# Layer statistics from one interleaved pass, and the first residual made by VectorE straight from PSUM

## The chip, the cores and the metric

The kernel runs on one core of a Trainium2 chip. The metric is the device time of one execution in microseconds (us). In the texts and profile rows PE is TensorE's matrix multiply and PEld its weight load, DVE is VectorE, ACT is ScalarE, POOL is GpSimd, SP is SyncE.

## What is computed

A batch of 32 graphs, each with 256 nodes of 256 features, goes through four graph layers. Each layer has a residual and a layer norm over the 256 features of a node:

```
x = _layernorm(x + _L0_gnn_ref(x, adj, W, b))            # adj @ (x W + b), divided by the row sums of adj
x = _layernorm(x + _L1_gnn_ref(x, adj, kernel))          # relu((adj @ x) kernel) * mask
x = _layernorm(x + _L2_gnn_ref(x, adj, kernel, bias))    # relu(normalized (adj + I) @ x kernel + bias)
x = _layernorm(x + _L3_gnn_ref(x, adj, Wv, bv, aw, ab, Wk, bk))   # attention weights, two hops, relu

def _layernorm(x, axis=-1, eps=1e-05):
    m = jnp.mean(x, axis=axis, keepdims=True)
    v = jnp.var(x, axis=axis, keepdims=True)
    return (x - m) / jnp.sqrt(v + eps)
```

So each graph needs a mean and a variance per node four times, once per layer.

## The kernel before

A graph lies in SBUF as a tile of 128 partitions by C = 512 columns: each partition holds two nodes, node t = 0 in columns 0 to 255 and node t = 1 in columns 256 to 511. `nodes(tile)` is that tile seen as (partition, t, feature). Four graphs, the slots g = 0 to 3, are in flight together, and eight groups of four follow each other. Products are made to nearly full precision from a high and a low half of every operand (`_hi`, `_lo`), three matmuls for each pair: ACT copies the high half out, and DVE or POOL subtracts it to get the low half.

The order of the work is written out by hand, separately for each engine: `first_iteration()`, then a loop over `iteration(k)`, which does layers 2 and 3 of group k interleaved with layers 0 and 1 of group k + 1 (and the first product of group k + 2), and then `last_iteration(k)`. Every engine runs its list strictly in order, and semaphores join the engines. An engine also waits on a semaphore of its own where an operation reads what one shortly before has written (`st_ready`, `mv_ready`, `rinv0_ready`, `z2_ready`).

PSUM holds four `ring` tiles, one per slot, and two `pair` tiles of two banks each. PE writes layer 0's second product (`s2`) of slot g into `pair[g % 2]`, with column F holding the row sums of adj. `s2` of slots 2 and 3, `s8a` and `s8b` of slot 0 (layer 3) and the first `s1` products write the same banks again, and so must wait until layer 0's result has been taken out of them. Before the change ACT's `z0` takes it out.

The steps around the change, per slot:

- **Layer 0's residual.** DVE `sums0` (L993, L994) takes the row sums and their reciprocal `rinv`. ACT `z0` (L495) reads the product from `pair`, scales it by `rinv` and writes X1, two operations of 256 columns. POOL `y0` (L759) adds X1 to X0, one operation of 512 columns.
- **Statistics, for each of the four layers.** DVE `statistics` (L975): two `bn_stats` of 256 columns, one per node, 6 words each. DVE `moments` (L982): two `bn_aggr`, which join those words to mean and variance. DVE `variance_eps` (L987, L988): adds eps and negates the mean. Then POOL `power` (L766) raises to -0.5, and POOL or ACT normalizes.
- Other names in the rows: `from_ring` (L966), `h_lo_part` (L970), `xd_lo` (L1020), `x1_lo` (L1015), `alpha_lo_part` (L998) and `p2_lo` (L1002) make low halves; `leaky` is L1041, `mask_of_x1` L1006, `y1`, `y2b` and `y3` (L1011, L1033, L1067) are the other residuals; `q` (L1054), `y2` (L1028) and `z3` (L1062) are products taken from PSUM with a per-node scale, two operations of 256 columns.

## Time and profile before

| | us |
|---|---|
| median of 3 runs (609.42 to 612.31) | 609.57 |
| the profiled execution's own time | 607.73 |
| its span, first to last instruction | 605.7 |

| engine | busy us | share of the span | instructions |
|---|---|---|---|
| PE | 544.7 | 90% | 4044 |
| PEld | 512.8 | 85% | 4044 |
| DVE | 557.7 | 92% | 1597 |
| ACT | 425.2 | 70% | 937 |
| POOL | 466.8 | 77% | 575 |

Busy time is the time in which an engine has an instruction open. DVE and PE instructions overlap their neighbours' ends, so what an instruction takes out of its engine's time is the distance from its start to the next one's start, which the view in order of time shows. A stretch of the loop repeats every 70.5 us; the rows below use seven such stretches.

### The profile page before, as it was taken

Reading aid. Unit: us, or ns where it says so; the run is one execution under the profiler, and the core shown is the slowest. Engines: PE = TensorE matmul, PEld = TensorE weight load, DVE = VectorE, ACT = ScalarE, POOL = GpSimd, SP = SyncE. Lnnn points to the kernel's source line nnn. Section 1 sums busy time; section 2 is a strip of 40 time slices with the busy share of each in tenths; the row PEclk is TensorE's granted clock in tenths of the full one; section 3 lists DMA queues with packets and bytes.
Section 4 is the critical chain, followed back from the end, with each engine's and each line's share of the span. In section 5 each row is a group of like instructions: output and inputs, shape, how many; then the busy total and the mean of one; then the engine's idle time right before and its main releaser. Section 6 shows DMA issues by size and latency. Waiting matters only on the chain.

```text
span 605.7 us, 12633 instructions
## 1 busy us (share of the span) xinstructions
PE 544.7 (90%) x4044; PEld 512.8 (85%) x4044; DVE 557.7 (92%) x1597; ACT 425.2 (70%) x937; POOL 466.8 (77%) x575
## 2 busy tenths in 40 slices
PE   5688999999989999999998999899999999987983
PEld 5577988999889988999888999899889998886873
DVE  3789999999999999999999999999999999999766
ACT  5467887488856878578873878658785778756653
POOL 3798789788987789878897788977898787873243
PEclk9979999999999999999999999999999999999998
DMA  8623101430132300323014211313003200101001
GB/s 291 221 59 112 41 18 46 142 120 25 35 104 69 139 17 17 113 95 104 17 49 125 104 52 35 104 69 139 17 17 106 102 36 2 54 18 70 1 1 69
DMA packets 25223, 44.73 MB, mean 74 GB/s; under 512 B 3184, under 2 KB 3824, under 8 KB 25200
## 3 DMA queue, kind: packets, MB, share of 16 engines
q1 hardware_dynamic: 24336, 43.79, 22.0%
q10 hardware_dynamic: 864, 0.66, 0.3%
q8 instruction: 12, 0.20, 0.1%
q14 instruction: 11, 0.09, 0.1%
HBM read 36.05 MB, written 8.39 MB: 73 GB/s over the span
## 4 chain that ended last, share of the span: by engine, by line
DVE 56%; PE 28%; issue 7%; POOL 4%; DMA 2%; ACT 2%; DVEq 0%; ACTq 0%; POOLq 0%
DVE stats L975 10%; PE pair L259 6%; DVE nod_lo L1020 5%; PE pair L261 5%; PE pair L260 5%; PE ring L259 4%; DVE ring L1062 4%; DVE fea_lo L966 4%; PE ring L261 4%; PE ring L260 4%; DVE P L1054 4%; DVE powin L987 3%; DVE tmp L1041 3%; DVE X L1067 3%; DVE nod_lo L1015 3%
## 5 line engine op out<-in xcount | busy, mean ns | idle before, releaser
L766 POOL TENSOR_TENSOR rstd<-powin,minus_half 128x2 f32<-128x2 f32 (+1 forms) x128 | 105.0, 821 | 71.1 <-DVE nmean L988 71.1
L565 ACT ACTIVATE X<-X,nmr,rstd 128x256 f32<-128x256 f32 x192 | 103.7, 593 | 33.8 <-POOL nmr L775 33.7
L975 DVE BATCH_NORM_STATS2 stats<-X 128x6 f32<-128x256 f32 x256 | 94.3, 411 | 1.6 <-POOL X L759 1.2
L259 PE MATMUL ring<-adj_hi,nod_lo 128*128 128x256 f32 x256 | 74.8, 292 | 12.8 <-DVE X L1067 8.2
L259 PE MATMUL ring<-W_hi,fea_lo 128*128 128x256 f32 x256 | 72.4, 283 | 1.5 <-DVE fea_lo L966 1.4
L260 PE MATMUL ring<-adj_lo,nod_hi 128*128 128x256 f32 x256 | 72.8, 285 | 0.0
L261 PE MATMUL ring<-adj_hi,nod_hi 128*128 128x256 f32 x256 | 72.8, 284 | 0.0
L261 PE MATMUL ring<-W_hi,fea_hi 128*128 128x256 f32 x256 | 71.7, 280 | 0.0
L260 PE MATMUL ring<-W_lo,fea_hi 128*128 128x256 f32 x256 | 71.4, 279 | 0.0
L486 ACT ACTIVATE fea_hi<-ring 128x512 fp32r<-128x512 f32 x96 | 54.9, 588 | 16.5 <-PE ring L321 11.3
L486 ACT ACTIVATE h_hi<-P 128x512 fp32r<-128x512 f32 x32 | 20.3, 633 | 65.7 <-DVE P L1054 65.7
L966 DVE TENSOR_TENSOR fea_lo<-ring,fea_hi 128x512 fp32r<-128x512 f32 x96 | 63.3, 679 | 1.8 <-ACT fea_hi L486 1.8
L259 PEld LDWEIGHTS ring<-adj_hi,nod_lo 128*128 128x128 f32 x256 | 49.2, 192 | 16.2 <-DVE nod_lo L1020 11.9
L259 PE MATMUL pair<-WB_hi,fea_lo 128*128 128x512 f32 x128 | 53.6, 419 | 9.5 <-DVE h_lo L1002 9.5
L788 POOL TENSOR_TENSOR tmp<-tmp,adj_in 128x512 f32<-128x512 f32 x32 | 44.0, 1385 | 14.2 <-ACT tmp L550 14.2
L796 POOL TENSOR_TENSOR h_lo<-P,h_hi 128x512 fp32r<-128x512 f32 x32 | 39.3, 1229 | 17.5 <-ACT h_hi L486 16.7
L261 PE MATMUL pair<-WB_hi,fea_hi 128*128 128x512 f32 x128 | 50.7, 396 | 0.0
L260 PE MATMUL pair<-WB_lo,fea_hi 128*128 128x512 f32 x128 | 50.7, 396 | 0.0
L781 POOL TENSOR_SCALAR X<-X,nmean,rstd 128x256 f32<-128x256 f32 x64 | 45.8, 725 | 5.7 <-POOL rstd L766 5.7
L259 PEld LDWEIGHTS ring<-W_hi,fea_lo 128*128 128x128 f32 x256 | 48.2, 188 | 2.4 <-issue 1.3
L754 POOL TENSOR_TENSOR adj_lo<-adj_in,adj_hi 128x512 fp32r<-128x512 f32 x32 | 40.8, 1293 | 11.7 <-ACT adj_hi L486 11.7
L261 PEld LDWEIGHTS ring<-adj_hi,nod_hi 128*128 128x128 f32 x256 | 49.5, 193 | 0.0
(110 smaller groups left out, 2166.2 us busy)
## 6 DMA issues: line engine op xcount, KB each, us to landing
adj_in<-adjT_dram SPq DMA_DIRECT2D x64, 256.0 KB, 3.2
xT_in<-xT_dram SPq DMA_DIRECT2D x32, 256.0 KB, 3.5
X<-x_dram SPq DMA_DIRECT2D x32, 256.0 KB, 2.6
out_dram<-X SPq DMA_DIRECT2D x32, 256.0 KB, 2.0
P<-wk_dram SPq DMA_DIRECT2D x3, 256.0 KB, 8.1
P<-w_dram SPq DMA_DIRECT2D x2, 256.0 KB, 7.8
X<-bk_dram SPq DMA_DIRECT2D x3, 128.0 KB, 7.8
P<-w_dram ACTq DMA_DIRECT2D x1, 256.0 KB, 3.8
```

The source lines that it names most:

```text
L259: mm(o, lhs(1, t, i), rhs(0, t), start=t == 0, stop=False)
L260: mm(o, lhs(0, t, i), rhs(1, t), start=False, stop=False)
L261: last = mm(o, lhs(0, t, i), rhs(0, t), start=False, stop=t == 1)
L486: return nc.scalar.activation(dst, src, ACT.Copy)
L565: last = nc.scalar.activation(nodes(X[min(l + 1, 3)][g])[:, t, :], nodes(X[l][g])[:, t, :], ACT.Identity, scale=rstd[l][g][:, t:t + 1], bi ...
L754: tt(adj_lo[g][:, :], adj_in[g][:, :], adj_hi[g][:, :], ALU.subtract).then_inc(adj_ready, 1)
L766: tt(rstd[l][g][:, 0:n], powin[l][g][:, 0:n], minus_half[:, 0:n], ALU.pow).then_inc(rstd_ready[l], 1)
L781: last = ts(nodes(X1[g])[:, t, :], nodes(X0[g])[:, t, :], nmean[0][g][:, t:t + 1], rstd[0][g][:, t:t + 1], ALU.add, ALU.mult)
L788: tt(tmp[g][:, :], tmp[g][:, :], adj3_in[g][:, :], ALU.mult).then_inc(al_ready, 1)
L796: tt(mixed(h_lo[g])[:, :, 0:F], nodes(P1[g]), mixed(h_hi[g])[:, :, 0:F], ALU.subtract).then_inc(Q_lo_ready, 1)
L966: tt(fea_lo[g][:, :], ring[g][:, :], fea_hi[g][:, :], ALU.subtract).then_inc(ready, 1)
L975: last = nc.vector.bn_stats(stats[l][g][:, 6 * t:6 * t + 6], nodes(X[l][g])[:, t, :])
```

## The change

`by_turns(tile)` shows the two nodes of a tile interleaved: feature 0 of node 0, feature 0 of node 1, feature 1 of node 0, and so on. One `bn_stats` over those 512 columns writes six words: count, mean and sum of squared deviations of its elements with even numbers, and the same three of those with odd numbers. With this view the even ones are node 0 and the odd ones node 1, so nothing has to be joined: `moments` is gone, and `variance_eps` reads the words directly, with the division by F in the operation that adds eps. Layer 0's residual becomes `y0` on DVE, two operations per slot that multiply the PSUM product by `rinv` and add X0 in place; ACT's `z0` and POOL's `y0` are gone, and PE waits for `y0_done` where it waited for `z0_ready`.

```diff
+        def by_turns(tile):
+            return tile[:, 0:C].rearrange("p (t f) -> p f t", t=2)
...
             def s2(g, kn):
...
                 if g >= 2:
-                    pe.wait_ge(z0_ready, count(g - 2, kn))
+                    pe.wait_ge(y0_done, count(g - 2, kn))
...
-            def z0(g, kn):
-                act.wait_ge(rinv0_ready, count(g, kn))
-                for t in range(2):
-                    last = nc.scalar.activation(nodes(X1[g])[:, t, :], pair[g % 2][:, t, 0:F], ACT.Identity,
-                                                scale=rinv[g][:, t:t + 1])
-                last.then_inc(z0_ready, 1)
...
-            def y0(g, kn):
-                pool.wait_ge(xb_ready, count(g, kn))
-                pool.wait_ge(z0_ready, count(g, kn))
-                tt(X0[g][:, :], X0[g][:, :], X1[g][:, :], ALU.add).then_inc(y_ready[0][g], 1)
...
             def statistics(l, g, k):
-                dve.wait_ge(y_ready[l][g], k + 1)
-                for t in range(2):
-                    last = nc.vector.bn_stats(stats[l][g][:, 6 * t:6 * t + 6], nodes(X[l][g])[:, t, :])
-                last.then_inc(st_ready[l], 1)
-
-            def moments(l, g, k):
+                if l == 0:
+                    dve.wait_ge(y0_done, count(g, k))
+                else:
+                    dve.wait_ge(y_ready[l][g], k + 1)
+                nc.vector.bn_stats(stats[l][g][:, :], by_turns(X[l][g])).then_inc(st_ready[l], 1)
+
+            def variance_eps(l, g, k):
                 dve.wait_ge(w0_ready, 1)
                 dve.wait_ge(st_ready[l], count(g, k))
-                for t in range(2):
-                    last = nc.vector.bn_aggr(mv[l][g][:, 2 * t:2 * t + 2], stats[l][g][:, 6 * t:6 * t + 6])
-                last.then_inc(mv_ready[l], 1)
-
-            def variance_eps(l, g, k):
-                dve.wait_ge(mv_ready[l], count(g, k))
-                ts(powin[l][g][:, 0:2], mv[l][g][:, 1:4:2], EPS, None, ALU.add)
-                ts(nmean[l][g][:, :], mv[l][g][:, 0:4:2], -1.0, None, ALU.mult).then_inc(nm_ready[l], 1)
+                ts(powin[l][g][:, 0:2], stats[l][g][:, 2:6:3], 1.0 / F, EPS, ALU.mult, ALU.add)
+                ts(nmean[l][g][:, :], stats[l][g][:, 1:6:3], -1.0, None, ALU.mult).then_inc(nm_ready[l], 1)
...
+            def y0(g, kn):
+                dve.wait_ge(rinv0_ready, count(g, kn))
+                dve.wait_ge(xb_ready, count(g, kn))
+                for t in range(2):
+                    half = nodes(X0[g])[:, t, :]
+                    last = stt(half, pair[g % 2][:, t, 0:F], rinv[g][:, t:t + 1], half, ALU.mult, ALU.add)
+                last.then_inc(y0_done, 1)
```

In the lists of work all 128 calls of `moments` go (32 graphs, four layers), and the calls of `z0` and of POOL's `y0` go. DVE's `y0(g, k + 1)` stands a few places behind `sums0(g, k + 1)`. The rest of every list keeps its order.

The part of DVE's loop in which layer 2 of group k and layer 0 of group k + 1 begin, before (`powin<-pair` and `rinv<-pair` are `sums0`, `ring<-ring,rstd` is `y2`, `X<-ring,X` is `y2b`, the number behind a name is the slot):

```order
L982 BN_AGGR mv_0<-stats_0 128x2 x2
L993 TENSOR_SCALAR powin_0<-pair 128x2
L994 RECIPROCAL rinv<-pair 128x2
L987 TENSOR_SCALAR powin_0<-mv_0 128x2
L988 TENSOR_SCALAR nmean_0<-mv_0 128x2
L1028 SCALAR_TENSOR_TENSOR ring<-ring,rstd_1,b_bc 128x256 x2
L1028 SCALAR_TENSOR_TENSOR ring<-ring,rstd_2,b_bc 128x256 x2
L1033 SCALAR_TENSOR_TENSOR X_1<-ring,X_1 128x512
L993 TENSOR_SCALAR powin_1<-pair 128x2
L994 RECIPROCAL rinv<-pair 128x2
L975 BN_STATS stats_1<-X_1 128x6 x2
```

The same part with the change:

```order
L961 TENSOR_SCALAR powin_0<-pair 128x2
L962 RECIPROCAL rinv<-pair 128x2
L955 TENSOR_SCALAR powin_0<-stats_0 128x2
L956 TENSOR_SCALAR nmean_0<-stats_0 128x2
L969 SCALAR_TENSOR_TENSOR X_0<-pair,rinv,X_0 128x256 x2
L1004 SCALAR_TENSOR_TENSOR ring<-ring,rstd_1,b_bc 128x256 x2
L1004 SCALAR_TENSOR_TENSOR ring<-ring,rstd_2,b_bc 128x256 x2
L1009 SCALAR_TENSOR_TENSOR X_1<-ring,X_1 128x512
L961 TENSOR_SCALAR powin_1<-pair 128x2
L962 RECIPROCAL rinv<-pair 128x2
L950 BN_STATS stats_1<-X_1 128x6
L969 SCALAR_TENSOR_TENSOR X_1<-pair,rinv,X_1 128x256 x2
```

The joins `BN_AGGR` are gone, a `BN_STATS` stands once where it stood twice, and `X<-pair,rinv,X` (the new `y0`) stands ahead of the next slots' `y2` (slot 0) and behind the statistics that follow `sums0` (slot 1).

The part of DVE's loop in which layers 2 and 0 of the later slots meet, before (`P<-pair,bk_bc` is layer 3's `p0`, `nod_lo` is `x1_lo`):

```order
L975 BN_STATS stats_1<-X_1 128x6 x2
L1033 SCALAR_TENSOR_TENSOR X_3<-ring,X_3 128x512
L1015 TENSOR_TENSOR nod_lo<-X_0,nod_hi 128x512
L975 BN_STATS stats_3<-X_3 128x6 x2
L1037 TENSOR_TENSOR P_1<-pair,bk_bc 128x516
L1002 TENSOR_TENSOR h_lo<-pair,h_hi 128x2x256
L982 BN_AGGR mv_3<-stats_3 128x2 x2
L982 BN_AGGR mv_1<-stats_1 128x2 x2
L987 TENSOR_SCALAR powin_3<-mv_3 128x2
L988 TENSOR_SCALAR nmean_3<-mv_3 128x2
```

With the change:

```order
L950 BN_STATS stats_1<-X_1 128x6
L1009 SCALAR_TENSOR_TENSOR X_3<-ring,X_3 128x512
L991 TENSOR_TENSOR nod_lo<-X_0,nod_hi 128x512
L950 BN_STATS stats_3<-X_3 128x6
L1013 TENSOR_TENSOR P_1<-pair,bk_bc 128x516
L978 TENSOR_TENSOR h_lo<-pair,h_hi 128x2x256
L955 TENSOR_SCALAR powin_3<-stats_3 128x2
L956 TENSOR_SCALAR nmean_3<-stats_3 128x2
```

Two `BN_AGGR` rows of two operations each are gone between the low half `h_lo` and the eps operation; no operation has come in here.

POOL's list at the start of the loop, before (`rstd` is `power`, `nmr` is `mean_scale`, `X<-X,nmean,rstd` is `norm0`):

```order
L775 TENSOR_TENSOR nmr_0<-nmean_0,rstd_0 128x2
L759 TENSOR_TENSOR X_0<-X_0 128x512
L754 TENSOR_TENSOR adj_lo<-adj_in,adj_hi 128x512
L766 TENSOR_TENSOR rstd_1<-powin_1,minus_half 128x2
L775 TENSOR_TENSOR nmr_1<-nmean_1,rstd_1 128x2
L759 TENSOR_TENSOR X_1<-X_1 128x512
L766 TENSOR_TENSOR rstd_0<-powin_0,minus_half 128x4
L781 TENSOR_SCALAR X_0<-X_0,nmean_0,rstd_0 128x256 x2
```

With the change:

```order
L756 TENSOR_TENSOR nmr_0<-nmean_0,rstd_0 128x2
L740 TENSOR_TENSOR adj_lo<-adj_in,adj_hi 128x512
L747 TENSOR_TENSOR rstd_1<-powin_1,minus_half 128x2
L756 TENSOR_TENSOR nmr_1<-nmean_1,rstd_1 128x2
L747 TENSOR_TENSOR rstd_0<-powin_0,minus_half 128x4
L762 TENSOR_SCALAR X_0<-X_0,nmean_0,rstd_0 128x256 x2
```

The two `X<-X` additions (`y0` of slots 0 and 1) are gone, so that `power` of layer 0 follows at once on `mean_scale` of layer 2's slot 1.

## Rows read from the trace of the kernel before

**Rows 1.** The page: span, busy time of each engine, chain by engine.

```profile
span 605.7 us, 12633 instructions
...
PE 544.7 (90%) x4044; PEld 512.8 (85%) x4044; DVE 557.7 (92%) x1597; ACT 425.2 (70%) x937; POOL 466.8 (77%) x575
...
DVE 56%; PE 28%; issue 7%; POOL 4%; DMA 2%; ACT 2%; DVEq 0%; ACTq 0%; POOLq 0%
```

**Rows 2.** Windows, one a loop turn: busy us (count) of each engine.

```profile
core 0: us, PE busy (x) PEld busy (x) DVE busy (x) ACT busy (x) POOL busy (x), PEclk, DMA share, GB/s
...
247.20:317.70 70.50, 66.69 (x506) 63.26 (x505) 68.11 (x197) 52.30 (x116) 59.50 (x73) 1.00 0.23 74
...
sum 493.30, PE 465.37 PEld 439.50 DVE 474.43 ACT 366.29 POOL 412.76; mean PE 66.48 PEld 62.79 DVE 67.78 ACT 52.33 POOL 58.97
```

**Rows 3.** Lines of DVE by form: count | busy us, mean ns | idle before.

```profile
L975 DVE BATCH_NORM_STATS2 stats<-X 128x6 f32<-128x256 f32 x256 | 94.3, 411 | 1.6 <-POOL X L759 1.2
L966 DVE TENSOR_TENSOR fea_lo<-ring,fea_hi 128x512 fp32r<-128x512 f32 x96 | 63.3, 679 | 1.8 <-ACT fea_hi L486 1.8
...
L987 DVE TENSOR_SCALAR powin<-mv 128x2 f32<-128x2 f32 x128 | 35.0, 273 | 1.1
...
L982 DVE BATCH_NORM_AGGREGATE mv<-stats 128x2 f32<-128x6 f32 x256 | 29.7, 158 | 3.2 <-issue 0.2
...
L1054 DVE SCALAR_TENSOR_TENSOR P<-pair,rinv,P 128x256 f32<-128x256 f32 x64 | 27.6, 471 | 0.4
```

**Rows 4.** The same view, more operations with every operand in SBUF.

```profile
L1020 DVE SCALAR_TENSOR_TENSOR nod_lo<-X,rstd,nod_hi 128x256 fp32r<-128x256 f32 x64 | 46.2, 763 | 0.5 <-ACT nod_hi L527 0.4
...
L1041 DVE SCALAR_TENSOR_TENSOR tmp<-tmp 128x512 f32<-128x512 f32 x32 | 31.1, 972 | 1.5 <-ACT tmp L544 0.6
...
L998 DVE TENSOR_TENSOR alpha_lo<-tmp,alpha_hi 128x512 fp32r<-128x512 f32 x32 | 29.2, 928 | 0.0
L1015 DVE TENSOR_TENSOR nod_lo<-X,nod_hi 128x512 fp32r<-128x512 f32 x32 | 28.4, 889 | 2.1 <-ACT nod_hi L486 2.1
...
L1006 DVE TENSOR_SCALAR mask<-absum 128x2 f32<-128x2 f32 x32 | 13.1, 410 | 0.0
```

**Rows 5.** DVE in order of time, 285 to 296 us: start us, us, operation.

```profile
285.57 0.23 DVE L982 BATCH_NORM_AGGREGATE mv<-stats 128x2 f32<-128x6 f32 x2
285.72 0.12 DVE L993 TENSOR_SCALAR powin<-pair 128x2 f32<-128x2 f32 x1
...
286.12 0.74 DVE L975 BATCH_NORM_STATS2 stats<-X 128x6 f32<-128x256 f32 x2
286.78 0.86 DVE L1028 SCALAR_TENSOR_TENSOR ring<-ring,rstd,b_bc 128x256 f32<-128x256 f32 x2
287.55 0.23 DVE L982 BATCH_NORM_AGGREGATE mv<-stats 128x2 f32<-128x6 f32 x2
287.82 0.23 DVE L987 TENSOR_SCALAR powin<-mv 128x2 f32<-128x2 f32 x1
...
289.89 0.67 DVE L1033 SCALAR_TENSOR_TENSOR X<-ring,X 128x512 f32<-128x512 f32 x1
290.48 1.50 DVE L1015 TENSOR_TENSOR nod_lo<-X,nod_hi 128x512 fp32r<-128x512 f32 x1
...
294.78 0.74 DVE L975 BATCH_NORM_STATS2 stats<-X 128x6 f32<-128x256 f32 x2
295.62 0.25 DVE L982 BATCH_NORM_AGGREGATE mv<-stats 128x2 f32<-128x6 f32 x2
295.79 0.81 DVE L987 TENSOR_SCALAR powin<-mv 128x2 f32<-128x2 f32 x1
```

**Rows 6.** POOL in order of time, 290 to 296 us.

```profile
290.15 1.29 POOL L759 TENSOR_TENSOR X<-X 128x512 f32<-128x512 f32 x1
...
295.28 1.29 POOL L759 TENSOR_TENSOR X<-X 128x512 f32<-128x512 f32 x1
```

**Rows 7.** Waits over the whole span: total us, times, longest.

```profile
PE pair L259 <- ACT X L495: 4.6, 2, 2.3
```

More of the change, by code:

```diff
@@ L87, in build @@
         alpha_hi, alpha_lo = slots("alpha_hi", C, FR), slots("alpha_lo", C, FR)
-        stats = [slots(f"stats{l}_", 12) for l in range(4)]
-        mv = [slots(f"mv{l}_", 4) for l in range(4)]
+        stats = [slots(f"stats{l}_", 6) for l in range(4)]
         nmean = [slots(f"nmean{l}_", 2) for l in range(4)]
@@ L114, in build @@
         h_hi_ready, h_ready = sem("h_hi_ready"), sem("h_ready")
-        deg_ready, z0_ready = sem("deg_ready"), sem("z0_ready")
-        y_ready = [sem4(f"y{l}_ready") for l in range(4)]
+        deg_ready, y0_done = sem("deg_ready"), sem("y0_done")
+        y_ready = {l: sem4(f"y{l}_ready") for l in (1, 2, 3)}
         st_ready = [sem(f"st{l}_ready") for l in range(4)]
-        mv_ready = [sem(f"mv{l}_ready") for l in range(4)]
         nm_ready = [sem(f"nm{l}_ready") for l in range(4)]
@@ L280, in s1 @@
                 elif kn == 1:
-                    pe.wait_ge(z0_ready, count(2 + g // 2, 0))
+                    pe.wait_ge(y0_done, count(2 + g // 2, 0))
                 product([h_bank(g)[:, 0:N], h_bank(g)[:, N:2 * N]], cols((xT_hi, xT_lo), g),
@@ L329, in s8a @@
                 elif not last:
-                    pe.wait_ge(z0_ready, count(2, k + 1))
+                    pe.wait_ge(y0_done, count(2, k + 1))
                 product([pair[0][:, i, 0:FA] for i in range(2)], cols(fea, g),
@@ L337, in s8b @@
                 elif not last:
-                    pe.wait_ge(z0_ready, count(3, k + 1))
+                    pe.wait_ge(y0_done, count(3, k + 1))
                 product([pair[1][:, i, :] for i in range(2)], cols(fea, g),
@@ L814, in first_iteration @@
                     diag_sum(g, 0)
-                y0(0, 0)
                 xT_lo_part(0, 1)
-                for g in (1, 2):
-                    y0(g, 0)
                 xT_lo_part(1, 1)
@@ L824, in first_iteration @@
                 norm0(1, 0)
-                y0(3, 0)
                 power(0, 2, 0)
@@ L857, in iteration @@
                 mean_scale(2, 0, k)
-                y0(0, k + 1)
                 adj_lo_part(3, k + 1)
@@ L861, in iteration @@
                 mean_scale(2, 1, k)
-                y0(1, k + 1)
                 power(0, 0, k + 1)
@@ L867, in iteration @@
                 diag_sum(0, k + 1)
-                y0(2, k + 1)
                 if ahead:
@@ L872, in iteration @@
                 mean_scale(2, 3, k)
-                y0(3, k + 1)
                 power(0, 1, k + 1)
@@ L1098, in first_iteration @@
                 first_x_bias(0)
+                y0(0, 0)
                 sums0(1, 0)
                 first_x_bias(1)
+                y0(1, 0)
                 attention_constants()
@@ L1103, in first_iteration @@
                 first_x_bias(2)
+                y0(2, 0)
                 statistics(0, 0, 0)
-                moments(0, 0, 0)
                 variance_eps(0, 0, 0)
                 statistics(0, 1, 0)
-                moments(0, 1, 0)
                 variance_eps(0, 1, 0)
@@ L1112, in first_iteration @@
                 first_x_bias(3)
+                y0(3, 0)
                 x1_lo(0, 0)
                 statistics(0, 2, 0)
-                moments(0, 2, 0)
                 mask_of_x1(0, 0)
@@ L1140, in first_iteration @@
                 y1(3, 0)
-                moments(1, 2, 0)
                 mask_of_x1(3, 0)
@@ L1159, in iteration @@
                 h_lo_part(3, k + 1)
-                moments(2, 0, k)
                 sums0(0, k + 1)
                 variance_eps(2, 0, k)
+                y0(0, k + 1)
                 for g in (1, 2):
@@ L1167, in iteration @@
                 statistics(2, 1, k)
+                y0(1, k + 1)
                 sums0(2, k + 1)
-                moments(2, 1, k)
                 variance_eps(2, 1, k)
+                y0(2, k + 1)
                 statistics(0, 0, k + 1)
@@ L1173, in iteration @@
                 y2b(2, k)
-                moments(0, 0, k + 1)
                 sums0(3, k + 1)
                 variance_eps(0, 0, k + 1)
+                y0(3, k + 1)
                 statistics(2, 2, k)
                 y2(3, k)
-                moments(2, 2, k)
                 variance_eps(2, 2, k)
@@ L1203, in iteration @@
                 leaky(1, k)
-                moments(0, 3, k + 1)
                 y1(0, k + 1)
@@ L1227, in iteration @@
                 y1(2, k + 1)
-                moments(1, 1, k + 1)
                 alpha_sum(0, k)
@@ L1238, in iteration @@
                 alpha_inverse(1, k)
-                moments(1, 2, k + 1)
                 q(1, k)
@@ L1254, in iteration @@
                 z3(1, k)
-                moments(3, 0, k)
                 y3(1, k)
@@ L1270, in iteration @@
                 xd_lo(3, k + 1)
-                moments(3, 2, k)
                 y3(3, k)
@@ L1302, in last_iteration @@
                 p2_lo(0, k)
-                moments(2, 3, k)
                 variance_eps(2, 3, k)
@@ L1336, in last_iteration @@
                 z3(1, k)
-                moments(3, 0, k)
                 y3(1, k)
@@ L1341, in last_iteration @@
                 z3(2, k)
-                moments(3, 1, k)
                 y3(2, k)
@@ L1346, in last_iteration @@
                 z3(3, k)
-                moments(3, 2, k)
                 y3(3, k)
```

23 lines of the change are left out of this document (removed).

## The prediction

> **What bounds the kernel now.** I read the page first [rows 1]. Two engines are nearly full: DVE is busy 92% of the 605.7 us span and PE 90%. The chain of work that ended last runs 56% over DVE and 28% over PE, so DVE sets the end about two times out of three that one of the two does. A mean over the span hides the loop, so I cut seven stretches of 70.5 us, one for each turn, and read busy time by stage [rows 2]. In a turn DVE is busy 67.8 us, PE 66.5, POOL 59.0 and ACT 52.3. The granted TensorE clock is 1.00 there, its upper level of 2.4 GHz, so no change of clock is to be had. A turn therefore has 2.7 us in which DVE is not busy and 4.0 us in which PE is not. The second number is a ceiling: whatever DVE saves, a turn can't become more than 4.0 us shorter without PE doing less, and the change takes nothing from PE. ACT and POOL have room, so what the change takes from them counts only where somebody waits for them.
>
> What a DVE instruction costs its engine is not its busy time, because neighbours overlap. I read it from the view in order of time as the distance between starts [rows 5]. The two statistics operations start at 286.12 and the next operation at 286.78: 0.66 us for the pair. The two joins start at 285.57, the next at 285.72: 0.15 us. A 512-column operation starts at 289.89, the next at 290.48: 0.59 us. A pair of 256-column operations from PSUM starts at 286.78, the next at 287.55: 0.77 us.
>
> The same view shows two kinds of lost time. Where an operation waits for the one just before it, there is a gap: from the joins at 287.55 to the eps operation 0.27 us pass instead of 0.15, and from the statistics at 294.78 to their joins 0.84 instead of 0.66. And some operations are much longer than their like. The low half at 290.48 takes 1.50 us where another of 512 columns takes 0.68 [rows 3, 5]; POOL's addition runs from 290.15 to 291.44 at that time [rows 6]. The eps operation at 295.79 takes 0.81 us where the others of two columns take 0.16, and POOL's addition runs from 295.28 to 296.57. So DVE operations with all operands in SBUF are held while POOL works on SBUF.
>
> **The statistics.** Per slot and layer two operations of 256 columns become one of 512. In a form with no hidden costs it takes what the 512-column operations take: 0.59 to 0.60 us instead of 0.66. By busy time the rows give the same picture: 411 ns for 256 columns and 679 ns for 512 [rows 3] make 268 ns for 256 more columns, 1.047 ns per column, so 679 ns instead of two times 411. The joins go, 0.15 us. Together 0.21 us for each of the 16 slots and layers of a turn: **3.4 us a turn less**. The variance now needs a multiplication by 1/F, but in the operation that adds eps anyway: nothing.
>
> No row shows a DVE operation that takes every column from another place than the column before. Its cost is bounded by 679 ns (full rate) and by twice the time per column, 679 + 512 x 1.047 = 1215 ns. I take full rate: it is the nearest row in operation and size, the per-column step of 1.047 ns lies between two different operations and so looks like the engine's own, and the view alternates between only two contiguous runs. The other end is a rival below. The Trainium skill speaks against this choice: "SBUF — State Buffer", section "Door 1: The DMA port swizzle", says that SBUF reads at full bandwidth only if consecutive accesses hit the same 16-byte line at least twice, which interleaved nodes 1 KB apart never do. "Vector Engine (DVE) Microarchitecture Reference", section 5.2, gives 1.73 ns per column with one input hopping on every element against 1.054 contiguous, but adds that a one-input operation alternating between two regions ran at full rate. By the 1.73 the operation would be 0.34 us longer than in my sum (an estimate from that page); by the remark it would not be. No row here can decide it.
>
> **The joins' waits.** In the turn from 247.2 to 317.7 us I count five places where the eps operation directly follows its joins, with about 0.12 us of gap, and three where the joins directly follow their statistics, with about 0.17. That is 1.1 us. In the new order one place is left in a turn where eps directly follows its statistics. Saved: **0.9 us a turn**.
>
> **The first residual on DVE.** It is the form of `q`, which multiplies a PSUM product by `rinv` and adds an SBUF half, 471 ns per operation [rows 3]. A pair takes 0.77 us of DVE [rows 5]; four slots: **3.1 us a turn more**, and 0.1 for the wait on `rinv`. It reads one operand from SBUF and one from PSUM, and `q`'s mean of 471 shows no holding by POOL. Behind it in DVE's list stand `y2` and `y2b` of layer 2's next slots, which PE and ACT need for layer 3, so these come up to 0.8 us later per slot; ahead of it there are places where DVE idles for `s2` anyway. What was PE's wait for ACT's copy, 4.6 us in two places [rows 7], lies in the first stretch; there DVE's `y0` of slot 0 has to wait for the load of X0, which `z0` did not, and slot 1's comes sooner. I take 0 for the first stretch as a whole, between 2 less and 2 more.
>
> **POOL and ACT.** ACT loses 64 operations, POOL 32 additions of 1.29 us: 41 us. Their own time is covered by DVE and PE. But POOL's additions hold DVE up. Lower bound: the excess of DVE's held operations over their undisturbed like is (763 - 471) x 64 + (972 - 679) x 32 + (928 - 679) x 32 + (889 - 679) x 32 + (410 - 158) x 32 + (273 - 158) x 128 ns = 65.6 us [rows 3, 4], in 466.8 us of POOL work, 0.14 us for one of POOL; for 41 us that is 5.8, or 0.7 a turn. Upper bound: the two cases above cost 0.82 and 0.65 us in one turn [rows 5, 6], 1.5 a turn. Other POOL work moves up into the place and will do some of the holding again. I take **1.1 us a turn less**.
>
> **The sum.** A turn: -3.4 - 0.9 + 3.1 + 0.1 - 1.1 = -2.2 us of DVE; seven turns -15.4. PE is nearly as full, so I let the part of it arrive that corresponds to DVE's share of the chain, 56 of 84, two thirds: -10.3. The last iteration has eight slots and layers of statistics and no `y0`; DVE there works in single steps with both gaps, so 8 x 0.21 plus some 0.8 of gaps: -2.5. Sum -12.8. Against the profiled execution's own 607.73 us that makes 594.9; against the median of 609.57, which is 1.84 higher, **597** (596.8 rounded).
>
> A measurement of this kernel can tell about 0.5%, 3 us, from no change.
>
> **Rival 1, the reading by turns is slow.** The one operation replaces two, but each column comes from elsewhere. At the bound of 1215 ns, 128 operations bring 68.6 us; all lies on DVE, which becomes the sole bound, and the savings of 17.9 (15.4 and 2.5) then count in full: 609.6 + 50.7 = 660. The point from which it decides is 17.9 / 128 = 0.14 us per operation, 27% more per column. For it: no such view is in the kernel before. Against it: the one rate of all DVE rows. By the skill's 1.73 ns it would be 636 (an estimate). Chance 0.12.
>
> **Rival 2, the DVE work only changes place.** `y0` costs 3.1 and the statistics give 3.4; if POOL's other work holds DVE as long as before and the gaps of the joins turn into waits for PE or ACT, a turn is 0.2 us shorter and the time 608. For it: the two large terms nearly cancel, and PE has a list of its own with waits. Against: the gaps are in the rows. Chance 0.09.
>
> **Rival 3, `y0` stands in the way.** The additions of DVE work all lie in one part of a turn, that of [rows 5] and the few us before it, among layer 2's residuals, and half of the savings lie elsewhere. If POOL's relief stays out there too, this part grows by 3.1 - 8 x 0.21 - 0.5 = 0.9 us a turn; if it sets the turn's length: +6, 616. It decides from the point where the part outgrows what DVE idles there. Chance 0.05.
>
> **Rival 4, everything arrives.** PE's waits are mostly DVE's doing, POOL's relief is at its upper bound (0.4 more a turn) and the first stretch gives 2: -15.4 - 2.8 - 2.5 - 2 = -22.7, 587. The ceiling of 4.0 us a turn allows it. Chance 0.12.
>
> **The numbers.** My forecast has 0.62 and covers 590 to 606. Faster by over 0.5%: 0.62 + 0.12 = 0.74. Within: 0.09. Slower: 0.12 + 0.05 = 0.17. The range from 586 to 610 leaves out rivals 1 and 3 and a rest below, 0.2 together.
>
> **What would show it.** Right: statistics rows of about 680 ns and 128 of them, no join rows, `y0` at about 470 ns, DVE busy 66 us or less of a turn of 69, fewer long operations among those of [rows 4]. Wrong: statistics rows well above 820 ns, DVE busy 99% (rival 1); turns of 70.3 us with the same number of long operations (rival 2); PE or ACT waiting for `y2b` or for `y0` (rival 3). If PE is busy 97% of a turn and DVE idles more, the DVE sum was right and PE took the rest.

## The result, and the profile after

The changed kernel takes **606.45 us** (median of 20 runs; 603.86 to 609.93 but for one of 1341.85, more than twice any other, which the comparison leaves out), the kernel before 610.02 beside it (20 runs, 608.49 to 612.65). The ratio is 0.9938, 95% interval 0.9921 to 0.9956: about 3.8 us faster where 12.8 were forecast. The profiled execution took 605.59 us, against 607.73.

The page of the changed kernel, the lines that answer to [rows 1]:

```profile
span 603.8 us, 12217 instructions
...
PE 546.8 (91%) x4044; PEld 513.2 (85%) x4044; DVE 551.5 (91%) x1277; ACT 402.5 (67%) x873; POOL 429.5 (71%) x543
...
DVE 43%; PE 29%; POOL 10%; issue 8%; ACT 6%; SPq 1%; DMA 1%; DVEq 0%; ACTq 0%; POOLq 0%
```

320 DVE instructions are gone, ACT lost 23 us and POOL 37, and DVE became only 6.2 us less busy. The windows of the changed kernel by turn, as in [rows 2] (length, then busy us of PE, PEld, DVE, ACT, POOL):

```profile
245.30:315.60 70.30, 67.11 (x506) 63.26 (x506) 67.50 (x158) 49.61 (x109) 54.98 (x69) 1.00 0.24 75
...
sum 493.70, PE 467.96 PEld 440.40 DVE 469.55 ACT 345.30 POOL 377.27; mean PE 66.85 PEld 62.91 DVE 67.08 ACT 49.33 POOL 53.90
```

DVE is busy 67.1 us of a turn and not 66 or less, and the turn is as long as it was: 70.5 us in the mean of seven here (493.70 us), 70.5 in [rows 2] (493.30 us). DVE's lines by form in the changed kernel (count, busy us, mean ns, idle before), which answer to [rows 3, 4]:

```profile
L950 DVE BATCH_NORM_STATS2 stats<-X 128x6 f32<-128x512 f32 x128 | 89.3, 702 | 0.4
...
L996 DVE SCALAR_TENSOR_TENSOR nod_lo<-X,rstd,nod_hi 128x256 fp32r<-128x256 f32 x64 | 53.0, 871 | 1.3 <-ACT nod_hi L521 1.0
L955 DVE TENSOR_SCALAR powin<-stats 128x2 f32<-128x2 f32 x128 | 32.2, 252 | 1.5
L974 DVE TENSOR_TENSOR alpha_lo<-tmp,alpha_hi 128x512 fp32r<-128x512 f32 x32 | 28.2, 900 | 0.0
...
L969 DVE SCALAR_TENSOR_TENSOR X<-pair,rinv,X 128x256 f32<-128x256 f32 x64 | 27.8, 475 | 0.4
...
L991 DVE TENSOR_TENSOR nod_lo<-X,nod_hi 128x512 fp32r<-128x512 f32 x32 | 26.8, 838 | 1.0 <-ACT nod_hi L487 1.0
L1017 DVE SCALAR_TENSOR_TENSOR tmp<-tmp 128x512 f32<-128x512 f32 x32 | 26.1, 817 | 1.7 <-ACT tmp L538 1.5
...
L982 DVE TENSOR_SCALAR mask<-absum 128x2 f32<-128x2 f32 x32 | 13.8, 432 | 0.0
```

The new operations are as forecast: the single statistics operation is at nearly full rate (702 ns) and `y0` (L969) takes 475. But the holding by POOL is hardly less. With the formula of the prediction the excess is (871 - 471) x 64 + (817 - 679) x 32 + (900 - 679) x 32 + (838 - 679) x 32 + (432 - 158) x 32 + (252 - 158) x 128 ns = 63.0 us, where it was 65.6. `leaky` (L1017) and the eps operation (L955) became shorter, and `xd_lo` (L996), the low halves for layer 2's first product, longer, 871 ns instead of 763.

**Where the time went, by pieces.** The first `q` of each group marks a turn (first row `P<-pair,rinv,P` of DVE in order of time; before 105.55, 176.96, ... 528.87, 584.86). For every kernel of this study the table has the start of the first one, the six turns from it to the seventh, the mean of one, the rest up to the end of the span, and the granted clock of the first and the last piece; in the six turns it is 1.00 everywhere. `q` can slide against PE's list by a microsecond or two, and the seventh `q` belongs to a turn in which PE has no `s1` to do. So the last two columns give the turns by PE's own list, from the start of the first matmul of `s6` of slot 0 (layer 2's second product) to the next: the mean of six turns (from 60.53 to 484.95 us before, from 59.70 to 484.21 after), and the seventh turn, which has neither PE's `s1` nor POOL's work for a group after the next. Where the two ways differ, PE's list is the better one. The names are those of the experiments below.

| kernel | first `q` at | six turns | one turn | rest | span | clock, first and rest | six turns by PE, one | seventh by PE |
|---|---|---|---|---|---|---|---|---|
| before | 105.6 | 423.3 | 70.6 | 76.8 | 605.7 | 0.95, 0.97 | 70.7 | 66.9 |
| after | 104.2 | 423.8 | 70.6 | 75.8 | 603.8 | 0.97, 0.96 | 70.8 | 66.0 |
| e1, statistics alone | 107.1 | 417.0 | 69.5 | 77.3 | 601.4 | 0.95, 0.94 | 69.9 | 65.0 |
| e2, `y0` alone | 109.9 | 438.3 | 73.1 | 78.0 | 626.2 | 0.94, 0.94 | 73.6 | 67.6 |
| e3, columns in order | 106.2 | 421.0 | 70.2 | 75.7 | 602.9 | 0.95, 0.96 | 70.3 | 65.7 |
| e4, two POOL steps last | 104.8 | 422.9 | 70.5 | 75.8 | 603.4 | 0.95, 0.97 | 70.6 | 65.9 |
| e5, low halves first | 107.2 | 421.8 | 70.3 | 77.1 | 606.1 | 0.95, 0.95 | 70.7 | 65.7 |
| e6, after, less PE work | 103.4 | 412.4 | 68.7 | 74.1 | 589.9 | 0.95, 0.94 | 68.9 | 64.2 |
| e7, before, less PE work | 104.5 | 418.4 | 69.7 | 74.1 | 597.0 | 0.97, 0.96 | 69.8 | 66.5 |
| e8, two POOL steps split | 105.4 | 412.3 | 68.7 | 78.6 | 596.3 | 0.98, 0.93 | 68.9 | 65.9 |
| e10, one POOL step last | 107.5 | 416.0 | 69.3 | 75.8 | 599.3 | 0.94, 0.96 | 69.6 | 66.3 |
| e9, statistics alone and the split | 104.3 | 408.5 | 68.1 | 75.8 | 588.6 | 0.97, 0.97 | 68.1 | 65.0 |

The six turns, where I expected most of the gain, got none: 423.3 us before, 423.8 after, and by PE's list 424.4 and 424.5. What the profiled execution gained is 1.9 us. By PE's list 0.8 of it lie ahead of the first turn (60.5 and 59.7 us), and that is less than kernels with the same instructions differ in: e4, e8 and e10 have only POOL's list in another order, and their first turn begins at 60.3, 60.4 and 61.9. Another 0.9 lie in the seventh turn (66.88 and 65.95 us), and there the kernels sort themselves: the two with the DVE work of before (before, e7) need 66.9 and 66.5, the six with that of the change and all of PE's work 65.7 to 66.3, e1 and e9 65.0. The last 0.2 lie behind it. So something of the saving did arrive, once, where PE and POOL have less to do.

**Who waits.** PE's waits in the six turns of the kernel before (105.55 to 528.87 us: us in total, times, longest):

```profile
PE pair L259 <- DVE h_lo L1002: 8.0, 6, 1.3
PE ring L259 <- DVE X L1067: 7.6, 6, 1.3
PE pair L259 <- DVE P L1054: 3.8, 8, 0.9
PE ring L259 <- POOL h_lo L796: 2.1, 6, 0.4
PE pair L259 <- issue: 1.6, 4, 0.5
```

The same of the changed kernel (104.17 to 528.00 us):

```profile
PE ring L260 <- DVE X L1043: 7.7, 6, 1.3
PE pair L260 <- DVE fea_lo L939: 5.2, 12, 0.5
PE pair L260 <- DVE P L1030: 3.9, 8, 0.9
PE pair L260 <- DVE X L969: 2.4, 6, 0.4
PE ring L260 <- POOL h_lo L777: 2.0, 6, 0.3
```

These short lists are the whole of what DVE and POOL can give as long as PE's own work stays as it is. PE's busy time in the same stretch and the waits add up to its length: 400.1 + 23.1 of 423.3 before, 402.6 + 21.2 of 423.8 after. The waits fell by 1.9 us in six turns, 0.3 a turn. One is gone, 1.3 us a turn, that of `s8b(3)` for `p2_lo(2)` (L1002), which stands late in DVE's list and profits from all that was saved ahead of it. `s2(3)` waits at the same place as before: 1.6 us in six turns, for which the profile names no releaser ("issue"), and now 2.4 for `y0` (L969). Two waits for low halves of x3T (L939) are new, 0.9 us a turn together: `s8a(3)`'s, which e1 below has as well and which is what is left of the one that went, and `s8a(0)`'s. The latter comes from `y0`. This is that part of DVE's list in order of time (start us, us, operation):

```profile
280.18 0.69 DVE L950 BATCH_NORM_STATS2 stats<-X 128x6 f32<-128x512 f32 x1
280.79 0.85 DVE L969 SCALAR_TENSOR_TENSOR X<-pair,rinv,X 128x256 f32<-128x256 f32 x2
...
281.84 0.86 DVE L969 SCALAR_TENSOR_TENSOR X<-pair,rinv,X 128x256 f32<-128x256 f32 x2
282.62 0.70 DVE L950 BATCH_NORM_STATS2 stats<-X 128x6 f32<-128x512 f32 x1
283.24 0.67 DVE L939 TENSOR_TENSOR fea_lo<-ring,fea_hi 128x512 fp32r<-128x512 f32 x1
```

PE's `s2(3)` starts at 281.80, when the `y0` of slot 1 has freed its banks, after a wait of 0.40 us; `s8a(0)` starts at 283.97 after a wait of 0.50, when the low half of x3T is made, which stands behind the `y0` of three slots. The same rows give the price of a statistics operation as the distance of starts: 280.18 to 280.79, 282.62 to 283.24, so 0.61 to 0.62 us.

The largest wait, 1.3 us a turn, stayed as it was, although DVE had less to do ahead of it. In it `s5(3)`, layer 2's first product of slot 3, waits for `y3` (L1043, before L1067), which takes layer 3's result out of the same `ring` tile; the expectations call the place the hand-over. DVE of the changed kernel there, and POOL:

```profile
263.67 0.71 DVE L950 BATCH_NORM_STATS2 stats<-X 128x6 f32<-128x512 f32 x1
264.30 2.84 DVE L996 SCALAR_TENSOR_TENSOR nod_lo<-X,rstd,nod_hi 128x256 fp32r<-128x256 f32 x2
267.06 0.68 DVE L1043 SCALAR_TENSOR_TENSOR X<-ring,X 128x512 f32<-128x512 f32 x1
...
264.14 1.30 POOL L736 TENSOR_TENSOR X<-X,b_bc 128x512 f32<-128x512 f32 x1
265.38 1.48 POOL L773 TENSOR_TENSOR xT_lo<-xT_in,xT_hi 128x512 fp32r<-128x512 f32 x1
```

`xd_lo(3)`, two operations that take 0.86 us elsewhere, runs for 2.84 us, while POOL makes `x_bias(1)` and `xT_lo(3)` for the group after the next. In the kernel before it was the same meeting, and less of it:

```profile
266.44 2.45 DVE L1020 SCALAR_TENSOR_TENSOR nod_lo<-X,rstd,nod_hi 128x256 fp32r<-128x256 f32 x2
```

So this operation grew by 0.4 us. Its end goes by POOL: it comes 0.28 us behind that of POOL's `xT_lo(3)` in both kernels (267.14 and 266.86 us after; 268.89 and 268.61 before, where `xT_lo(3)` starts at 267.14 and takes 1.47). DVE began it 0.16 us behind the start of `x_bias(1)` after the change and 0.56 before, and what it came earlier it waited longer. That is how time saved ahead of it was lost.

A second place where POOL holds DVE comes up in some turns only. Of the six turns by PE's list four take 70.3 to 70.4 us and two 71.6; before it was four of 70.2 to 70.5 and two of 71.4 and 71.7. In the long ones `s10(2)` waits 0.9 us for slot 0's `q`, and ahead of that `q` two operations of two columns take 2.5 us beside two POOL operations:

```profile
384.81 1.31 DVE L955 TENSOR_SCALAR powin<-stats 128x2 f32<-128x2 f32 x1
386.03 1.34 DVE L956 TENSOR_SCALAR nmean<-stats 128x2 f32<-128x2 f32 x1
...
384.79 1.30 POOL L736 TENSOR_TENSOR X<-X,b_bc 128x512 f32<-128x512 f32 x1
386.05 1.29 POOL L769 TENSOR_TENSOR tmp<-tmp,adj_in 128x512 f32<-128x512 f32 x1
```

One turn earlier, at 314.49, they take 0.53 and 0.16. Both kernels have two such turns, so this does not touch the comparison of the two; e5 has three, e4 two, e1, e3 and e9 one, e2, e6, e7, e8 and e10 none. What decides whether the operations meet is not shown.

### The profile page after: what moved, and what is told of

It reads as the page before. It is cut to its first block, busy times and chain, and to the rows that moved or that the text cites. A ratio compares the mean times of both kernels' runs of the same rounds, so it can differ in the third digit from the quotient of the medians.

```text
span 603.8 us, 12217 instructions
## 1 busy us (share of the span) xinstructions
PE 546.8 (91%) x4044; PEld 513.2 (85%) x4044; DVE 551.5 (91%) x1277; ACT 402.5 (67%) x873; POOL 429.5 (71%) x543
## 4 chain that ended last, share of the span: by engine, by line
DVE 43%; PE 29%; POOL 10%; issue 8%; ACT 6%; SPq 1%; DMA 1%; DVEq 0%; ACTq 0%; POOLq 0%
PE pair L260 7%; DVE nod_lo L996 6%; PE pair L262 6%; PE pair L261 6%; DVE stats L950 5%; DVE P L1030 3%; ACT X L559 3%; PE ring L260 3%; DVE ring L1038 3%; DVE X L969 3%; POOL rstd L747 3%; DVE ring L1004 3%; DVE powin L955 3%; PE ring L262 3%; PE ring L261 2%
## 5 line engine op out<-in xcount | busy, mean ns | idle before, releaser
L747 POOL TENSOR_TENSOR rstd<-powin,minus_half 128x2 f32<-128x2 f32 (+1 forms) x128 | 106.1, 829 | 107.1 <-DVE nmean L956 107.1
L950 DVE BATCH_NORM_STATS2 stats<-X 128x6 f32<-128x512 f32 x128 | 89.3, 702 | 0.4
L939 DVE TENSOR_TENSOR fea_lo<-ring,fea_hi 128x512 fp32r<-128x512 f32 x96 | 63.8, 680 | 4.3 <-ACT fea_hi L487 4.3
L769 POOL TENSOR_TENSOR tmp<-tmp,adj_in 128x512 f32<-128x512 f32 x32 | 46.7, 1470 | 15.9 <-ACT tmp L544 15.9
L996 DVE SCALAR_TENSOR_TENSOR nod_lo<-X,rstd,nod_hi 128x256 fp32r<-128x256 f32 x64 | 53.0, 871 | 1.3 <-ACT nod_hi L521 1.0
L260 PE MATMUL pair<-WB_hi,fea_lo 128*128 128x512 f32 x128 | 53.7, 419 | 0.2 <-DVE h_lo L978 0.2
L762 POOL TENSOR_SCALAR X<-X,nmean,rstd 128x256 f32<-128x256 f32 x64 | 48.1, 761 | 6.0 <-POOL rstd L747 6.0
L740 POOL TENSOR_TENSOR adj_lo<-adj_in,adj_hi 128x512 fp32r<-128x512 f32 x32 | 41.0, 1303 | 14.8 <-ACT adj_hi L487 14.8
L261 PEld LDWEIGHTS ring<-adj_lo,nod_hi 128*128 128x128 f32 x256 | 50.0, 195 | 0.0
```

What stands on the lines that cost most here:

```text
L260: mm(o, lhs(1, t, i), rhs(0, t), start=t == 0, stop=False)
L261: mm(o, lhs(0, t, i), rhs(1, t), start=False, stop=False)
L740: tt(adj_lo[g][:, :], adj_in[g][:, :], adj_hi[g][:, :], ALU.subtract).then_inc(adj_ready, 1)
L747: tt(rstd[l][g][:, 0:n], powin[l][g][:, 0:n], minus_half[:, 0:n], ALU.pow).then_inc(rstd_ready[l], 1)
L762: last = ts(nodes(X1[g])[:, t, :], nodes(X0[g])[:, t, :], nmean[0][g][:, t:t + 1], rstd[0][g][:, t:t + 1], ALU.add, ALU.mult)
L769: tt(tmp[g][:, :], tmp[g][:, :], adj3_in[g][:, :], ALU.mult).then_inc(al_ready, 1)
```

## The experiments

**Theory A**: PE paces the loop together with DVE. DVE's savings reach the end only where PE waits, and the change opened new waits of PE (`y0` ahead of the low half of x3T) in place of the one it closed. **Theory B**: DVE alone paces the loop, and the savings were given back to POOL's holding. The ratios below are to the kernel before, run beside each on the same chip.

### The two halves alone

e1 is the kernel before with the statistics part of the change alone, e2 with the `y0` part alone.

```diff
e1 (against before)
+                nc.vector.bn_stats(stats[l][g][:, :], by_turns(X[l][g])).then_inc(st_ready[l], 1)
...
-                moments(2, 0, k)
...
e2 (against before)
-                z0(0, k + 1)
...
+                y0(0, k + 1)
```

> Only the statistics part of the change, on the kernel before: one operation by turns, no joins; the residual stays with ACT and POOL. Theory A (PE paces the loop: 66.0 us of its own work in a turn of 70.3, DVE's savings pay only where PE has a gap that DVE causes): DVE has 5 us a turn less to do, but PE's gaps were 4.6 us, of which the 1.5 us one ahead of s8b goes and the 1.4 us one at the hand-over to s5 stays, so a turn is 1.5 to 2 us shorter and the time 596 to 599. Theory B (DVE paces the loop and POOL's holding ate the savings): DVE's 5 us a turn arrive less about 1 of holding, 580 to 585.

> Only the residual part of the change, on the kernel before: DVE's y0 from PSUM, with two statistics operations and joins as before. DVE has 3.1 us a turn more where it was busy 67.8 of 70.5, and POOL 5.2 less. Theory A: DVE now comes to about 70.5 us of work and PE's gaps grow: 618 to 628, so the two halves of the change nearly cancel. Theory B: POOL's relief gives back 1.1 to 1.5 us a turn, 612 to 618.

Measured: e1 597.84 us (595.51 to 603.24), ratio 0.9764 [0.9735, 0.9793]; e2 626.77 us, ratio 1.0243 [1.0214, 1.0273]. The statistics alone are worth 14 us, more than the 12.8 that I forecast for the whole, and `y0` on DVE costs 15; both medians are where Theory A had them. The product of the two ratios is 1.0001, the change has 0.9938: together they are 4 us better than one by one. The statistics part takes 3.9 us from DVE in a turn (3.0 and 0.9, below), and a turn of e1 is 0.9 us shorter by PE's list (1.1 by `q`); PE now has the largest share of the page's chain, and no longer DVE:

```profile
PE 547.4 (91%) x4044; PEld 515.6 (86%) x4044; DVE 540.0 (90%) x1213; ACT 425.5 (71%) x937; POOL 471.2 (78%) x575
...
PE 39%; DVE 29%; POOL 13%; issue 8%; ACT 7%; DMA 2%; POOLq 0%; ACTq 0%; DVEq 0%
```

PE's waits in its six turns (107.09 to 524.11 us) make 18.5 us, and the largest is still that of `s5` for `y3`:

```profile
PE ring L260 <- DVE X L1060: 7.8, 6, 1.3
PE pair L260 <- DVE P L1047: 3.3, 9, 0.9
PE pair L260 <- DVE fea_lo L967: 2.8, 6, 0.5
```

In e2 DVE's 3.1 us more a turn make the turn 2.9 us longer by PE's list (2.5 by `q`), and PE waits 32.8 us in its six turns (109.92 to 548.23 us), for seven groups of operations. Behind the 7.6 us for `y3` the largest are:

```profile
PE pair L259 <- DVE fea_lo L938: 7.2, 11, 0.8
PE pair L259 <- DVE alpha_lo L981: 5.0, 5, 1.0
PE pair L259 <- DVE h_lo L985: 4.9, 6, 1.1
```

The gain of 14 us is more than e1's loop shows: by PE's list 5.2 us in the six turns and 1.9 in the seventh. The profile of e1 was taken of its longest run (603.24 us, mean granted clock 0.984). One other run had that clock and took 602.97; the six with 0.987 to 0.990 took 595.5 to 598.1. The clock is full in the loop, so these 6 us may lie ahead of it and behind it; no profile of a quicker run of e1 is there to show it. e9 below, which has the same work on every engine and was profiled in a run at its median, is 2.4 us shorter there (61.1 us up to the first turn by PE's list and 53.7 behind the seventh, where e1 has 62.0 and 55.1). Where the rest went is not shown.

### The low halves ahead of the statistics

e5 is the changed kernel with two low halves of x3T moved up in DVE's list, to close the two new waits of PE.

```diff
-                statistics(0, 0, k + 1)
                 from_ring(0, x3T_hi_ready, k, x3T_ready)
+                statistics(0, 0, k + 1)
...
+                from_ring(3, x3T_hi_ready, k, x3T_ready)
                 x1_lo(1, k + 1)
                 variance_eps(0, 3, k + 1)
-                from_ring(3, x3T_hi_ready, k, x3T_ready)
```

> The changed kernel with two operations earlier in DVE's list: the low half of x3T of slot 0 ahead of layer 0's first statistics, and that of slot 3 ahead of the x1 low half of slot 1. PE has gaps of 0.66 and 0.51 us ahead of the products that read these. Theory A: they go in good part, 0.5 to 1.0 us a turn, 599 to 603. Theory B: the same DVE work in another order, 606 to 607.

Measured: 606.44 us, ratio 0.9925 [0.9894, 0.9956], no gain over the changed kernel. Theory A's number is missed, and Theory B's was right. PE's waits in the six turns of e5 (107.17 to 528.98 us), those that were not or not so before:

```profile
PE ring L260 <- DVE X L1043: 5.7, 6, 1.0
PE pair L260 <- DVE P L1030: 4.6, 9, 0.9
...
PE pair L260 <- DVE alpha_lo L974: 2.4, 3, 0.8
...
PE pair L260 <- DVE h_lo L978: 1.9, 3, 0.6
```

The 5.2 us for `fea_lo` are gone, and 2 of the 7.7 for `y3`; in their place come 2.4 for `alpha_lo`, 1.9 for `p2_lo` and 0.7 more for `q` (a third of the long turns), and the sum falls from 21.2 to 19.1. DVE is full there, so an operation that goes first sends another one back: by the order of one full engine a wait is mostly moved.

### PE with less to do

In e6 (from the changed kernel) and e7 (from the one before) `s8b` leaves out one of its three matmuls of each kind, high half by low half, so the attention's feature product has less precision: 16 matmuls of 512 columns, which start 0.23 to 0.24 us apart, so 3.8 us of PE a turn.

```diff
-                        mm(o, lhs(0, t, i), rhs(1, t), start=False, stop=False)
+                        if not short:
+                            mm(o, lhs(0, t, i), rhs(1, t), start=False, stop=False)
...
-                        lambda s, t: WB[s][:, t, :]).then_inc(s8b_done, 1)
+                        lambda s, t: WB[s][:, t, :], short=True).then_inc(s8b_done, 1)
```

> The changed kernel with the middle one of the three matmuls left out of every pair in s8b (high half of x3T by low half of WB), so that its result lacks that term: 16 matmuls of 512 columns less, 3.8 us of PE less in a turn; the other engines' lists are untouched. Theory A (PE paces the changed kernel): a turn gets shorter by about 2 us, until DVE's work (67.1 us busy, some of it held) bounds it: 590 to 594. Theory B (DVE paces it): 604 to 607.

> The same term left out of the kernel before. Theory A: before, DVE was as much of a bound as PE, so little comes of it, 605 to 609, and the ratio of the changed kernel to this one falls from 0.994 to about 0.975, which is what the DVE sum of the prediction gave. Theory B: 607 to 610, and the ratio stays at 0.994.

Measured: e6 591.84 us, ratio 0.9699 [0.966, 0.9738]; e7 600.6 us, ratio 0.985 [0.9809, 0.989]. e6 is where Theory A had it. e7 is 4 us below its range: PE paces the kernel before, too, in part. Still the pair bears on the question. With less PE work the change is worth 0.9699 / 0.985 = 0.985 (0.979 to 0.990 by both intervals), 9 us instead of 4, and six turns become 6.0 us shorter by it (418.4 to 412.4; by PE's list 5.5, 418.6 to 413.2), 0.9 to 1.0 a turn, where with the full PE work they became no shorter. DVE did save time, and PE's own work kept part of it from arriving. But neither kernel gets back the 30 us that PE has less (3.8 for each of eight groups): it is 14.6 from the changed kernel and 9.4 from the one before. In e6 PE waits 7.4 us in six turns for `p2_lo` again, the wait that the change had closed. DVE, with what holds it, paces the other part.

### POOL's steps out of the way

At the meeting of `xd_lo(3)` with two long POOL operations, e4 puts both of them last in POOL's turn, e10 only `x_bias(1)`, and e8 puts `x_bias(1)` last and `xT_lo(3)` far ahead. All start from the changed kernel.

```diff
e8 (e10: only the lines on x_bias; e4: xT_lo_part(3) goes last as well)
-                for g in (1, 2):
-                    power(1, g, k + 1)
+                power(1, 1, k + 1)
+                if ahead:
+                    xT_lo_part(3, k + 2)
+                power(1, 2, k + 1)
...
-                if ahead:
-                    x_bias(1, k + 2)
-                    xT_lo_part(3, k + 2)
...
-                    for g in (2, 3):
+                    for g in (1, 2, 3):
                         x_bias(g, k + 2)
```

> The changed kernel with POOL's addition of the bias for slot 1 and low half of xT for slot 3 moved behind the last power and mean_scale of layer 3. In the trace they stand exactly where DVE's two xd_lo of slots 2 and 3 take 2.84 us instead of 0.87, and PE then waits 1.3 us. Theory A: the gap at the hand-over shrinks by about 1.2 us a turn, 597 to 599. Theory B: DVE gets its 2 us a turn back, 593 to 596. If the two operations only hold other DVE operations where they now stand, 605 to 607.

> The changed kernel with POOL's bias addition for slot 1 behind the last mean_scale of layer 3, and the low half of xT for slot 3 far earlier, between two powers of layer 1 where POOL idled 1.45 us. With both operations late, DVE was no longer held at the hand-over but PE's gap moved to s1, which waited for that low half. Theory A: the gap at the hand-over now goes from 1.4 to about 0.4 us and none comes instead: 599 to 602. If the gap is not due to the holding but to DVE's and ACT's chain there: 605 to 607.

> Only one of the two moves in POOL's list on the changed kernel: the bias addition for slot 1 goes behind the last mean_scale, the low half of xT for slot 3 stays. It then runs about 1.3 us earlier, and DVE's two xd_lo are held once instead of twice. Theory A: PE's gap at the hand-over shrinks by what one holding costs, about 0.9 us a turn, and s1 isn't late: 599 to 602. If the low half just holds both operations as long as before: 605 to 607.

Measured: e4 605.95 us, ratio 0.9902 [0.987, 0.9933]; e10 600.01, 0.9828 [0.9795, 0.9861]; e8 596.68, 0.9777 [0.9744, 0.9809]. e10 is where Theory A had it, e8 is 2 us better than its range, and in e4 both theories' numbers are missed, and the time is that of the changed kernel: the holding is gone and nothing is gained. DVE and PE of e4 in order of time:

```profile
265.75 0.86 DVE L994 SCALAR_TENSOR_TENSOR nod_lo<-X,rstd,nod_hi 128x256 fp32r<-128x256 f32 x2
...
270.64 0.38 PE L260 MATMUL pair<-W_hi,xT_lo 128*128 128x256 f32 x1 [1.14 <-POOL xT_lo L773]
```

`xd_lo(3)` takes 0.86 us again, but PE's `s1` of slot 3 for the group after the next now waits 1.14 us for the `xT_lo(3)` that was put off. DVE is busy 393.8 us in e4's six turns instead of 405.9, and they are no shorter than 422.9. So DVE's time at this place is not what paces, which speaks against Theory B; the wait of PE is. In e8 `xT_lo(3)` is early enough for PE and away from `xd_lo`. PE's waits in the six turns of e8 (105.44 to 517.72 us):

```profile
PE pair L260 <- DVE fea_lo L938: 5.1, 12, 0.5
PE pair L260 <- DVE X L968: 2.5, 6, 0.4
PE pair L260 <- DVE P L1029: 2.4, 8, 0.3
PE ring L260 <- POOL h_lo L777: 2.0, 6, 0.4
```

The wait of `s5` for `y3` is no longer there and 12.0 us are left of 21.2; the mean turn is 1.8 us shorter by PE's list (1.9 by `q`). Of the 9.2 us of waits that went, 7.7 are the one for `y3` and 1.5 that for `q`, since e8 has none of the long turns. e10 has less of the holding left (`xd_lo(3)` takes 1.47 us). Its PE waits 1.3 us for `y3` in the six turns instead of 7.7, but 4.3 for `y0` instead of 2.4, 14.8 in all, and its turn is 1.2 us shorter by PE's list (1.3 by `q`).

### The columns in order

e3 is the changed kernel with the statistics operation reading the 512 columns one after another. What it takes as a node's mean is then that of the even or odd columns of both, so the layer norm is another one; the work is the same.

```diff
-                nc.vector.bn_stats(stats[l][g][:, :], by_turns(X[l][g])).then_inc(st_ready[l], 1)
+                nc.vector.bn_stats(stats[l][g][:, :], X[l][g][:, :]).then_inc(st_ready[l], 1)
```

> The changed kernel with the statistics operation reading the 512 columns in order instead of by turns, so that its two triples belong to even and odd features of both nodes and the result is not the layer norm; every instruction else is the same. The operation by turns takes 702 ns. If the 23 ns over the 679 ns of other 512-column operations are the price of hopping between the two nodes, it takes 679 here; if they belong to the operation, 702. Either way 0.02 us x 128 = 3 us of DVE at most, and under Theory A less arrives: 605 to 606.5.

Measured: 604.15 us, just below the range, ratio 0.9895 [0.9854, 0.9936], which overlaps that of the change. The group of the statistics in e3:

```profile
L950 DVE BATCH_NORM_STATS2 stats<-X 128x6 f32<-128x512 f32 x128 | 86.9, 683 | 0.4
```

Reading by turns costs 19 ns of 702, 3%, or 2.4 us of DVE in the whole kernel.

### The better half with the POOL steps split

e9 is e1 with e8's two moves: the statistics of the change, layer 0's residual left with ACT and POOL.

> The statistics part alone (the residual with ACT and POOL as before) with the same two moves in POOL's list. Theory A: the two effects add, as PE's gap at the hand-over is the same 1.4 us in both: 590 to 594. If POOL, busy 78% here, can't take the low half earlier without holding something else up: 597 to 599.

Measured: **590.84 us**, ratio 0.9676 [0.964, 0.9711], where Theory A had it. The page of e9:

```profile
PE 541.9 (92%) x4044; PEld 511.6 (87%) x4044; DVE 527.0 (90%) x1213; ACT 424.5 (72%) x937; POOL 470.2 (80%) x575
...
PE 57%; DVE 18%; POOL 14%; issue 5%; ACT 5%; DMA 1%; POOLq 0%; ACTq 0%; DVEq 0%
```

It beats both kernels, the one before by 3.2%, nearly 20 us. A turn is 68.1 us with 66.4 of PE in it and 1.6 of waits (9.7 in its six turns), and the chain is PE's: by DVE and POOL no more than those 1.6 us a turn are left to gain while PE's work stays as it is.

## Why the prediction came out as it did

**The direction, and rival 1.** Faster was right. The size was not: 3.8 us arrived of 12.8. 606.45 lies just above the 590 to 606 that my forecast covers and inside the wider range up to 610. The rate of the by-turns reading, taken as full against the longer bound, was right: 702 ns, against 683 in order. Rival 1's mechanism (660 us) is not there. The Trainium skill's rule in "SBUF — State Buffer", "Door 1: The DMA port swizzle", by which such reads lose bandwidth, does not show in this operation. The Trainium skill's remark in "Vector Engine (DVE) Microarchitecture Reference", section 5.2, that an operation with one input alternating between two regions runs at full rate, agrees with it but for the 19 ns.

**The statistics, 3.4 us a turn.** The form was right, the size a little high. The slot is 0.62 us and not 0.59 (19 of the 30 ns are the hopping, e3), so a slot and layer saves 0.66 + 0.15 - 0.62 = 0.19 us, 3.0 a turn.

**The joins' waits, 0.9.** Not tried alone. Where eps directly follows its statistics the gap is still there: in the changed kernel the statistics start at 267.80 and the eps operation at 268.61, 0.81 us instead of 0.62. One of the five places that I counted (295.62 to 295.79, 0.17 us) has hardly a gap, so the rows give 0.8 rather than 0.9.

**`y0`, 3.1 and 0.1.** The price was right (475 ns; a pair from 277.09 to 277.88, 0.79 us). Its place was costed at nothing, under "places where DVE idles for `s2` anyway", and this failed: `s8a(0)` now waits 0.5 us a turn for a low half behind it, `s2(3)` waits 0.4 for `y0` itself, and by the halves alone `y0` costs 15 us where the statistics bring 14. That is rival 3's mechanism, though at another reader than I named.

**POOL's holding, 1.1.** Of DVE's terms this one was mis-sized most. I took a share of the excess between two bounds; the rows after give 65.6 - 63.0 = 2.6 us, 0.3 a turn. POOL's other long operations moved up, and one of them sits on `xd_lo(3)`. e4, e8 and e10 show that the place of the same POOL work alone is worth from nothing to 1.8 us a turn.

**The sum.** With the measured sizes DVE's saving is -3.0 - 0.9 + 3.1 + 0.1 - 0.3 = -1.0 us a turn and not -2.2. e6 against e7 has 0.9 to 1.0. So Theory A stands, with the part of Theory B that e8 and e10 show: POOL's holding counts where it delays an operation that PE waits for.

**The step that failed** is the one after it, "I let the part of it arrive that corresponds to DVE's share of the chain, 56 of 84". Of -1.0 nothing that can be told arrived in the six turns. I took the 4.0 us in which PE is not busy for a ceiling only. They are a list of five or six waits, each ended by one operation of DVE or POOL. A saving counts if it brings that operation forward, and up to the length of that wait. The change closed one (1.3 us a turn), left the other large one as it was (1.3, its operation held by POOL), and opened two (0.9). DVE's share of the chain says nothing of this; e1's chain is 29% DVE and e2's 65%, with turns of 69.9 and 73.6 us.

**The last iteration, 2.5.** This failed as well. By PE's list the span behind the seventh turn is 0.2 us shorter (53.87 and 53.64 us), although DVE is busy 1.6 less there (39.7 and 38.2), and PE's longest waits in it are the same, 1.7, 1.5 or 1.4, 1.1 and 1.0 us. The profiled executions differ by 1.9 us, and the ratio says 3.8; from where the other 1.9 come is not shown.

**The rivals.** By what the profile shows rival 2 came nearest (the work only changes place, turns as long as before, 608 us), with a part of rival 3. Rival 4 asked for all to arrive, and e1 shows that even 3.9 us of DVE a turn bring 0.9.
